# Two row scatters in flight instead of three in the routing phase of a decoder layer

## The reference, cut to what matters

```python
def _L0_ffn_ref(x, gate_w, gate_b, w1_shared, w2_shared, w3_shared, w1_routed, w2_routed, w3_routed):
    logits = jnp.einsum('ed,btd->bte', gate_w, x)
    scores = jax.nn.sigmoid(logits) + gate_b
    weights, indices = jax.lax.top_k(scores, TOP_K)      # TOP_K = 4 of 16 experts
    weights = weights / weights.sum(-1, keepdims=True)
    shared_out = jax.nn.silu(x @ w1_shared) * (x @ w3_shared) @ w2_shared
    ...
    routed_out = jnp.einsum('bted,bte->btd', experts_out, router_probs)
    return shared_out + routed_out

x = x + _L0_attn_ref(_layernorm(x), ...)
x = x + _L0_xattn_ref(_layernorm(x), ..., ctx_2048, ctx_2048, 54)
x = x + _L0_ffn_ref(_layernorm(x), ...)
```

## Time and profile before

| | us |
|---|---|
| three runs, median (lowest, highest) | 844.42 (840.83, 850.3) |
| profiled execution, first to last instruction (span) | 847.7 |
| time beside that span, where the profiled execution is the slowest of the three | 2.6 |
| first scatter of rows starts, last one starts (from the span's start) | 258.98, 501.24 |
| barrier behind the routing phase passed | 512.4 |

### The profile page before, as it was taken

One profiled execution on the slowest core, in us unless ns is written; L12 is line 12 of the kernel. 1 busy time (PEld: TensorE's weight loads), 2 busy tenths in 40 slices (PEclk: granted clock), 3 DMA queues, 4 the chain that ended last, 5 costly groups with the idle time before them and its releaser, 6 DMA issues. The chain is left out here.

```text
span 847.7 us, 15795 instructions
## 1 busy us (share of the span) xinstructions
PE 664.4 (78%) x4034; PEld 555.8 (66%) x4034; DVE 569.3 (67%) x1747; ACT 402.3 (47%) x1136; POOL 459.9 (54%) x363
## 2 busy tenths in 40 slices
PE   1888679883578988785736355799999999999994
PEld 1777667763455656453524224699999999999993
DVE  5799769933667666452614665777777777777774
ACT  3866346211256545242322134555555555555552
POOL 3566665460005455535334550667777776777775
PEclk9999889997579999787958677999999999999997
DMA  9900001213125546622212353477777787787774
GB/s 295 290 23 26 26 13 38 87 51 118 44 100 192 190 139 236 240 72 100 73 65 88 130 180 103 75 124 130 133 132 133 127 134 125 130 140 126 140 113 57
DMA packets 77094, 100.38 MB, mean 118 GB/s; under 512 B 9744, under 2 KB 70304, under 8 KB 76448
## 3 DMA queue, kind: packets, MB, share of 16 engines
q0 software_dynamic: 26736, 37.64, 25.2%
q1 hardware_dynamic: 48096, 59.64, 22.7%
q10 hardware_dynamic: 2176, 2.10, 0.8%
HBM read 50.97 MB, written 52.95 MB: 123 GB/s over the span
## 5 line engine op out<-in xcount | busy, mean ns | idle before, releaser
L1562 POOL DMA_INDIRECT out_dram<-yw,xg x143 | 225.1, 1574 | 116.1 <-issue 61.0
L1184 POOL DMA_INDIRECT xs_scratch<-rows,slot x128 | 125.0, 977 | 172.6 <-issue 91.8
L1445 PE MATMUL cbank<-w_hi,xtc_hi 128*128 x286 | 107.4, 375 | 7.9 <-DVE xtc_lo L1457 7.8
L1445 PE MATMUL cbank<-w,stc_hi 112*128 (+1 forms) x572 | 111.9, 289 | 1.0 <-DVE stc_hi L1527 0.8
L1505 ACT ACTIVATE sgc<-hh 128x128 f32<-128x128 f32 x143 | 44.4, 311 | 129.8 <-DVE hh L1499 96.9
L1457 DVE TENSOR_TENSOR xtc_lo<-cbank,xtc_hi 128x256 fp32r<-128x256 f32 x143 | 60.6, 424 | 60.4 <-ACT xtc_hi L1452 49.1
L355 POOL TENSOR_TENSOR pv<-v_sb,pr 128x256 f32<-128x256 f32 (+7 forms) x32 | 68.5, 2154 | 58.1 <-DVE pr L344 39.8
L1445 PEld LDWEIGHTS cbank<-w,stc_hi 112*128 112x128 f32 (+1 forms) x572 | 92.9, 189 | 5.4 <-issue 3.6
L1445 PE MATMUL cbank<-w,xtc_hi 128*128 x286 | 93.2, 326 | 0.0
L1445 PE MATMUL cbank<-w_hi,xtc_lo 128*128 x286 | 92.5, 324 | 0.0
L1445 PEld LDWEIGHTS cbank<-w_hi,xtc_hi 128*128 128x128 f32 x286 | 54.0, 189 | 23.0 <-issue 11.0
(11 more groups left out here) (223 smaller groups left out, 1577.6 us busy)
## 6 DMA issues: line engine op xcount, KB each, us to landing
xg<-xs_scratch SPq DMA_DIRECT2D x143, 144.0 KB
w<-w13r_dram SPq DMA_DIRECT2D x8, 704.0 KB
w_hi<-ctx_t_dram SPq DMA_DIRECT2D x8, 512.0 KB
x_scratch<-x_all SPq DMA_DIRECT2D x16, 256.0 KB, 2.1
w_hi<-x_scratch SPq DMA_DIRECT2D x8, 512.0 KB, 5.7
out_dram<-w SPq DMA_DIRECT2D x16, 256.0 KB
w<-w2r_dram SPq DMA_DIRECT2D x4, 1024.0 KB
x_all<-x_dram SPq DMA_DIRECT2D x12, 256.0 KB
```

Source lines behind the costliest of these rows:

```text
L1184: nc.gpsimd.indirect_dma_start(t["xs"], bass.IndirectOffsetOnAxis(ap=slot[:, n % 2, k:k + 1].bitcast(U32), axis=0), rows[:, n % NROW, k // ...
L1445: last = nc.tensor.matmul(out, stationary, moving, start=j == 0, stop=j == len(pairs) - 1)
L1562: nc.gpsimd.indirect_dma_start(t["out"], bass.IndirectOffsetOnAxis(ap=xg[:, p, ID:ID + 1].bitcast(U32), axis=0), yw[:, p % YB, :], None, c ...
```

## The change

`FLY` goes from 3 to 2. The ring has two semaphores; scatter m now waits for the landing of scatter m - 2, and `rows_landed` looks at two semaphores. Nothing else is touched: the number of scatters, their sizes, their order and every other wait are the same.

```diff
 NROW, NX1, NX2, NX3 = 3, 3, 4, 3
 COEF = 9
 AHEAD_G = 2
-FLY = 3
+FLY = 2
 PIECES = 12
```

## The result

The ring of two took 822.2 us (median of 4, 816.7 to 836.7) against 847.4 us for the kernel before (median of 4, 840.8 to 850.3): ratio 0.968, 95% interval 0.963 to 0.974. It is 3.2% faster; slower by 0.8% was forecast.

What follows compares the result with a forecast made beforehand. The prediction took late PE signals, held up by bursts of scatters, to bound the routing phase. Quiet scatters 2.4 plus slow landings 9 made 11.4 us; 0.6 of it, +7 us, on 844.4 gave 851 us, range 840 to 862.

Steps and rivals of the forecast that it cites:

- What bounds the kernel: Routing phase, 253.4 us: no engine near full; finished PE steps reach their waiters microseconds late while GpSimd issues scatters back to back.
- four cases: Waits of DVE or ACT for PE in the routing phase, read as 4.8, 10.2, 7.3 and 3.4 us late, 26 us.
- The quiet scatter: Scatters in quiet bursts: a ring of two adds 0.02 us per scatter, 2.4 us in all.
- The lane's turn: Time from a scatter's start to the start of the scatter it releases: 2.57 us, against 2.53 available with two lanes.
- w: Time between a scatter's last packet and the start of the scatter it releases: zero to 0.58 us, taken at 0.45.
- The slow landings: Scatters landing slowly beside the other queue's loads and stores: about one step of 1.265 us lost per stretch, 9 us.
- How much reaches the end: Share of the bursts' 11.4 us growth that lengthens the kernel: 0.6, so +7 us.
- Relief: Rival, routing bursts: longer gaps between scatters let PE's late signals through; 843 us, 830 with all back; chance 0.12.
- hold of a microsecond or more: Wait of GpSimd for a landing, one per group ahead of the critical PE signal, supposed in pricing 843 us.
- Full pass: Rival: every burst's end is on the path and slow landings cost more; +11.4 to +20 us, 856 to 864; chance 0.20.
- No change: Rival: GpSimd's slack of 61.3 us takes up the bursts' growth; 844 to 847 us, centre 845; chance 0.23.
- What would show it: Signs expected in the changed kernel's profile: over 10 landing waits, quiet bursts 19.0 to 20.3 us, routing phase about 260 us.

Runs made afterwards that it cites:

- experiment 5: Unchanged copy of the ring of two, against the kernel before, on another chip: 810.5 us against 787.3, ratio 1.028.

## Why the prediction was wrong

*What bounds the kernel.* Right, and it was the useful part: signals of finished PE steps reach their waiters late while scatters are issued back to back. I read four cases and put them at 26 us, in two of which the waiter was itself busy for part of the time (ACT until 428.26, DVE until 470.26), so 23.4 us were idle. All such waits together are 79.5 us by the table, and the stretch is 58.6 us longer on the late chip than on the quick one with the same kernel (242.2 against 183.6).

*The quiet scatter.* The lane's turn was put at 2.57 us and is 2.71 to 2.74, so the loss is some 0.09 per quiet step and some 11 us in all if every step had it, not 2.4. The upper bound (w at most 0.58, 10 us) was nearly exact; I moved away from it only because zero stood at the other end, though zero was no measurement. What w consists of can be read in experiment 5, whose trace has the landing of every second scatter: the quickest lands 2.42 us after its start, the median one 2.48, and GpSimd starts the scatter that waited 0.27 us after the landing. This last term was not thought of, though the earlier trace rows show 0.30 us of idle time even ahead of a scatter that waits for nothing. The Trainium skill's fit ("DMA: Bandwidth & Descriptors", "Anatomy of one DMA — SWDGE (gpsimd) path") gave an estimate of 2.34 us for the landing. The trace agrees, with 2.42 to 2.48 us. But the prediction set the landing alone against the 2.53 us between starts; with the 0.27 us even the quickest takes 2.69.

*The slow landings.* Put at 9 us, they make the rest of 26.6, about 16 by subtraction; the four first, busy bursts grew by 17.1 us together, the four quieter ones by 9.5. The growth of the bursts was thus 11.4 forecast, 26.6 measured on the late chip and 31.1 on the quick one.

*How much reaches the end.* This is the step that failed. I took 0.6 of the growth and a plus sign. The two had to be kept apart: where no signal is late the growth goes wholly into the stretch (30.9 of 31.1 us), and the late signals are a cost of their own, which slower bursts buy back: from 79.5 to 35.3 us here. On the late chip stretch less bursts fell by 51 us (68.2 to 17.2) for 26.6 of growth; another 6 us went behind the last burst, where the time from its last scatter's start to the phase's end fell from 11.2 (501.24 to 512.4) to 5.3 us (475.0 to 480.3).

*The rivals.* Relief came about. Its mechanism is borne out, by the memsets too: with scatters further apart the signals get through. Its size was wrong: 843 was its middle, 830 its far end, and 822 lies beyond, because I had priced only the four waits that I had read out, less than a third of the 79.5 us. I gave it 0.12 on the ground that the gap grows by only 0.02 us. By the runs it grows by 0.09 on average in quiet stretches, and relief does not need a "hold of a microsecond or more": two memsets, which lengthen the quiet step by 0.11 us, already gain 1.2%. Full pass is what happens on a quick chip (+23 us between the medians, more than the 11.4 to 20 that it forecast). No change did not come about on either sort of chip; GpSimd's 61.3 us of waiting for DVE, which I took for slack, were themselves made by the late signals and are 1.4 us on a quick chip.

*What would show it.* Waits on landings in large number: yes, 72. Quiet bursts of 19.0 to 20.3 us: a little more, 20.9 and 21.1. Busy ones 1 to 2.5 us longer: 3.6 to 4.8. Phase of 260 us: no. `where_` and `prt` 2 to 4 us behind each burst's last scatter: `where_` still twice, 2.4 us behind the fifth and the sixth, but `prt` and the first `where_` came in mid-burst, and their late time fell, which was named as the sign of relief.

## What to carry to other kernels

Where an engine's waiter starts long after its producer's end and the lag ends with another engine's burst of GpSimd scatters, sum that lag over the phase first: it is a cost in its own right, and pacing the scatters may buy back more than it costs. Try the pace by itself (small memsets ahead of each scatter, two, four), since ring depth sets pace as a side effect and hides what worked. And measure such a kernel on more than one chip before believing the sign: here the ring of two is 3% faster on two and 3% slower on one, and of the versions run none beat the ring of two on late chips or the kernel before on quick ones.

## What the runs showed of the hardware that was not expected

The same program falls into two sorts of time. It takes 787 us on three chips and 842 to 847 in the four sets of runs elsewhere, and nearly all of the difference lies in the phase with back-to-back scatters: the attention phase (257.2 and 257.3 us) and the expert phase (334.6 and 334.4) are alike in the profile of the kernel after on its late chip and in that of the kernel before on a quick one.

```profile
0.00:257.30 257.30, 180.81 (x1056) 151.89 (x1057) 186.65 (x415) 122.47 (x253) 109.87 (x93) 0.88 0.29 94
257.30:450.00 192.70, 153.96 (x836) 102.82 (x834) 137.43 (x603) 91.70 (x156) 124.86 (x128) 0.93 0.53 186
450.00:784.40 334.40, 313.07 (x2145) 292.47 (x2145) 245.68 (x731) 188.43 (x730) 225.14 (x143) 0.97 0.70 121
```

This is the kernel before by stretch on a quick chip: 192.7 us of routing with the same 836 matmuls that took 253.4. PE's busy time differs as well, 171.2 us at a mean granted clock of 0.83 on the late chip against 154.0 at 0.93 here. But a lower clock is not what makes signals late: the ring of one had 0.73 on a quick chip and no late signal (1.7 us in the table).

```profile
256.50:640.00 383.50, 164.24 (x836) 110.06 (x833) 134.83 (x603) 91.90 (x155) 125.45 (x128) 0.73 0.27 93
```

It is PE's signals that are late, not all. Inside the bursts of the kernel before, on its late chip, ACT started 0.03 us after DVE's `neg` (L972) in all five waits for it. PE started 0.05 to 0.06 us after the step of ACT or DVE that it waited for in six of seven such waits (at L1013, L1031, L1084, L1167 and L1216), and 1.2 us after it in the seventh.

What a late chip has that delays signals, and whether it is GpSimd's descriptor work or the scatters' completions that stand in their way, stays open: pacing changes both at once, and no run told them apart. Nor was it tried whether the delay exists in an execution that is not profiled.

Deeper is not safer: on late chips each step of the ring from two to three to four costs about 3% (0.968, 1, 1.028, the last with an interval of 1.014 to 1.042), though each removes waits of GpSimd for landings.
